# One Trainium2 core, a vision tower kernel: state scan and routed experts as one stage, class key scores in the gate's product

## The reference, cut to what matters

```python
h = h + _L1_attn_ref(_layernorm(h), ...)     # ends in: hs by a scan over the batch axis, y = pad(h) * z; y @ w_out.T
def _L1_ffn_ref(x, W_qkv, b_qkv, W_gate, b_gate, W_experts, b_experts):
    qkv = (x @ W_qkv + b_qkv).reshape(B, S, 3, H, hd)          # 16 heads of 16
    attn = softmax(q k^T / 4) over all 513 tokens of an image
    gate = jax.nn.softmax(x @ W_gate + b_gate, axis=-1)
    top_g, top_i = jax.lax.top_k(gate, TOP_K)                   # 2 of 8
    moe_out = sum over the two of top_g * (x @ W_experts[e] + b_experts[e])
    return attn_out + moe_out
h = h + _L1_ffn_ref(_layernorm(h), ...)
```

## Time and profile before

| | us |
|---|---|
| median of 3 runs (lowest to highest) | 2109.86 (2108.89 to 2119.64) |
| profiled execution: time | 2123.18 |
| profiled execution: span, mean granted clock | 2121.5, 0.941 |
| state scan's result ready | 1310.4 |
| slot table done | 1523.0 |
| first expert product | 1532.9 |
| last bias addition of the expert stage | 1624.8 |

### The profile page before, as it was taken

How to read it: one execution, slowest core, us unless ns; L and a number is a source line. 1 busy time by engine, 2 the same in 40 slices (tenths; PEclk the granted TensorE clock), 3 DMA queues, 4 the chain that set the end, 5 groups by cost and what they waited for, 6 DMA issues and landing times. The chain is left out here.

```text
span 2121.5 us, 37207 instructions
## 1 busy us (share of the span) xinstructions
PE 1915.3 (90%) x10969; PEld 1211.2 (57%) x10969; DVE 1540.5 (73%) x4226; ACT 933.6 (44%) x2148; POOL 991.3 (47%) x1655
## 2 busy tenths in 40 slices
PE   7997997999899998999996994798797899999997
PEld 5886772333788887677774332788674233333332
DVE  3334896776577776899984885787665888898881
ACT  1112564555122222444442442344353277777777
POOL 3553564555333332333332110577444766666662
PEclk9997998999899999999998996899898599999999
DMA  4331667875100001990002001368764134434420
GB/s 132 114 118 39 155 168 182 167 157 109 45 1 1 1 1 71 412 387 1 1 1 61 9 9 30 105 156 232 181 212 140 28 84 97 96 93 93 101 67 27
DMA packets 242423, 216.77 MB, mean 102 GB/s; under 512 B 117762, under 2 KB 216100, under 8 KB 242116
## 3 DMA queue, kind: packets, MB, share of 16 engines
q1 hardware_dynamic: 232596, 188.26, 33.0%
q0 software_dynamic: 9648, 26.36, 3.8%
HBM read 109.35 MB, written 104.82 MB: 101 GB/s over the span
## 5 line engine op out<-in xcount | busy, mean ns | idle before, releaser
L2966 DVE TENSOR_REDUCE attend_mx<-ps 128x1 f32<-128x512 f32 x512 | 320.8, 681 | 38.5 <-PE ps L2620 37.4
L2763 ACT ACTIVATE attend_w<-ps 128x512 f32<-128x512 f32 x512 | 281.8, 596 | 96.9 <-PE ps L2634 94.6
L2620 PE MATMUL ps<-keep_x,keep_o 96*128 96x512 bf16 x512 | 209.3, 414 | 8.2 <-DVE attend_mx L2966 6.4
L2634 PE MATMUL ps<-keep_o,keep_x 99*128 99x512 bf16 x512 | 191.9, 384 | 2.7 <-ACT attend_w L2763 2.7
L2620 PEld LDWEIGHTS ps<-keep_x,keep_o 96*128 96x128 bf16 x512 | 50.2, 98 | 194.5 <-DVE attend_mx L2966 146.2
L981 POOL TENSOR_TENSOR keep_early<-keep_early,first_causal 128x128 f32<-128x128 f32 x256 | 112.9, 456 | 90.8 <-ACT keep_early L949 89.7
L1003 DVE SCALAR_TENSOR_TENSOR keep_early<-ps,first_causal 128x512 f32<-128x512 f32 (+3 forms) x256 | 114.0, 485 | 51.1 <-PE ps L885 46.6
L949 ACT ACTIVATE keep_early<-ps 128x512 f32<-128x512 f32 (+3 forms) x256 | 98.9, 437 | 88.6 <-PE ps L885 88.2
L2652 PE MATMUL ps<-attend_w,keep_early 128*17 128x512 f32 x1024 | 136.3, 601 | 0.0
L1216 PE MATMUL ps<-mlp_zT,keep_early 128*128 128x128 f32 x1056 | 128.0, 280 | 8.0 <-ACT mlp_zT L1258 8.0
L1216 PEld LDWEIGHTS ps<-mlp_zT,keep_early 128*128 128x128 f32 x1056 | 121.8, 194 | 16.0 <-ACT mlp_zT L1258 16.0
(11 more groups left out here) (376 smaller groups left out, 4559.4 us busy)
## 6 DMA issues: line engine op xcount, KB each, us to landing
sorted<-keep_x SPq DMA_DIRECT2D x3, 14720.0 KB, 75.2
tok_xin<-in_xk SPq DMA_DIRECT2D x64, 256.0 KB, 2.6
qk_parts<-qkv_parts SPq DMA_DIRECT2D x33, 384.0 KB, 3.2
qk_parts<-moe_parts SPq DMA_DIRECT2D x33, 384.0 KB, 3.2
keep_o<-qk_parts SPq DMA_DIRECT2D x16, 384.0 KB, 4.5
keep_x<-qk_parts SPq DMA_DIRECT2D x16, 384.0 KB, 5.6
moe_zs<-sorted SPq DMA_DIRECT2D x45, 128.0 KB, 2.4
sorted<-moe_zn POOLq DMA_DIRECT2D x42, 128.0 KB, 2.4
```

The source lines that it names most:

```text
L2620: nc.tensor.matmul(ps[:, MX + i % RING, :], qs[0:R, x.buf(0), h, t * P:(t + 1) * P], ks[0:R, x.buf(0), h, :], start=True, stop=True).then_ ...
L2634: nc.tensor.matmul(ps[:, SC + i % RING, :], ks[:, x.buf(2), HG * g + j, kt * P:(kt + 1) * P], qs[:, x.buf(2), HG * g + j, :], start=True, ...
L2763: nc.scalar.activation(w[:, j, kt % 2, :], ps[:, SC + (HG * k + j) % RING, :], ACT.Exp)\
L2966: nc.vector.tensor_reduce(mx[:, t, k:k + 1], ps[:, MX + (TB * k + t) % RING, :], AX, ALU.max)\
```

## The change

`pass_scan` and `pass_moe` become one pass, `pass_experts`. What it does:

- The scan's buffers are views of `env.o` and `env.x`. The products of a pair of tiles (`carry(p)`) and their addition (`carried(p)`) stand in the turns, one pair every second turn, directly ahead of the pair's statistics. Statistics and deviation work on a pair.
- GpSimd's `deviation` also makes -mean/deviation, and ScalarE normalizes (`normalize`) where VectorE did.
- The class keys times the weights of k and q give 32 columns beside the gate's 8: `class_weights` makes them once (24 instructions on TensorE), and the gate's product of 40 columns gives the class scores too. `class_scores`, `take_class` and `qkf` are gone; `env.cs` holds 40 columns a tile.
- q and k stay in PSUM, in two banks. ScalarE's `first_part` writes the first part from there, VectorE's `remainder` makes the rest from PSUM and that part in four pieces, ScalarE's `second_part` casts, GpSimd's `third` is as before. `v` has four buffers; `rest` and `parts` still two.
- `choose` and `places` read the expert numbers and a zero from PSUM (`IOTA`, `ZERO`), where they read SBUF.
- A projection runs one turn after its gate for i < 8, then two, then three (`projected`), with none in turns 8 and 16; before it was always three.
- The exponents of all tiles are taken at once after the slot table.
- SyncE copies v ahead of the parts. Of the 16 pieces, 8 stay in the turns (tiles 12 to 26, every second one), and 8 stand between the loads of the expert stage.

```diff
+def projected(i):
+    lag = 1 if i < 8 else 2 if i < 16 else 3
+    return None if i in (8, 16) or not 0 <= i - lag < NT else i - lag
 # SyncE
             for s, u, n in tiles():
-                sp.wait_ge(s_p2, s + 1)
-                sp.dma_start(io["qk_parts"]...).then_inc(s_out[u], 16)
                 sp.wait_ge(s_va, s + 1)
...
+                sp.wait_ge(s_p2, s + 1)
+                sp.dma_start(io["qk_parts"]...).then_inc(s_out[u], 16)
+                if s >= 12 and s % 2 == 0 and s < 28:
+                    piece = (s - 12) // 2
+                    env.heads.load_piece(sp, io, 0, piece // 4, piece // 4, piece % 4)
...
                 sp.dma_start(zs[j % NY], io["sorted"][bass.ds(row, P), :]).then_inc(s_zs[j % NY], 16)
+                if j >= 12 and j % 4 == 0 and j < 44:
+                    piece = (j - 12) // 4
+                    env.heads.load_piece(sp, io, 1, piece // 4, 2 + piece // 4, piece % 4)
 # ScalarE
+            def first_part(s):
+                u = s % 2
+                act.wait_ge(s_qk, s + 1)
+                if s == 0:
+                    act.wait_ge(s_kq0, 1)
+                past(act, s_p2, s - 1)
+                past(act, s_out[u], 16 * (s // 2))
+                for n in range(4):
+                    last = nc.scalar.activation(part_at(u, 0, n), ps[:, QK[u], n * P:(n + 1) * P], ACT.Identity, bias=bias_of(n))
+                last.then_inc(s_p0, 1)
+            for i in range(NT + 4):
+                if live(i):
+                    take_zT(i)
+                if i == 2:
+                    take_class_weights()
+                if live(i + 2):
+                    normalize(i + 2)
+                if projected(i - 1) is not None:
+                    second_part(projected(i - 1))
+                if projected(i) is not None:
+                    first_part(projected(i))
 # GpSimd
+            def deviation(p):
+                u, w = (p + 1) % 2, len(members(p))
+                ch = Chain(pool, c_rs, 3 * (p + 1))
+                pool.wait_ge(s_stat, p + 2)
+                past(pool, s_z, 2 * p - 1)
+                ch.link(nc.gpsimd.tensor_tensor(ve[:, u, 0:w], mv[:, u, 0:w, 1], env.eps[:, :].to_broadcast([P, w]), ALU.add))
+                ch.link(nc.gpsimd.tensor_tensor(rs[:, u, 0:w], ve[:, u, 0:w], env.mhalf[:, :].to_broadcast([P, w]), ALU.pow))
+                ch.link(nc.gpsimd.tensor_tensor(nm[:, u, 0:w], mv[:, u, 0:w, 0], rs[:, u, 0:w], ALU.mult))
+                nc.gpsimd.tensor_tensor(nm[:, u, 0:w], no[:, :].to_broadcast([P, w]), nm[:, u, 0:w], ALU.subtract).then_inc(s_rs, 1)
+            for i in range(NT + 4):
+                if i % 2 == 0 and (i + 2) // 2 < NP:
+                    deviation((i + 2) // 2)
+                if live(i - 2):
+                    scatter(i - 2)
+                if projected(i - 1) is not None:
+                    third(projected(i - 1))
 # VectorE
+            def remainder(s):
+                u = s % 2
+                dve.wait_ge(s_p0, s + 1)
+                past(dve, s_p2, s - 1)
+                for n in range(4):
+                    last = nc.vector.scalar_tensor_tensor(rest[:, u, n * P:(n + 1) * P], ps[:, QK[u], n * P:(n + 1) * P], bias_of(n),
+                                                          part_at(u, 0, n), ALU.add, ALU.subtract)
+                last.then_inc(s_rest, 1)
                 if live(i - 1):
                     choose(i - 1)
                 if live(i - 2):
                     places(i - 2)
+                if projected(i - 1) is not None:
+                    remainder(projected(i - 1))
+                if projected(i) is not None:
+                    value(projected(i))
+                if i % 2 == 0 and (i + 2) // 2 < NP:
+                    carried((i + 2) // 2)
+                    stats((i + 2) // 2)
```

More of the change, by code:

```diff
@@ L1830, in _ @@
             convolve(B - 1)
[L1833 to L1915, removed]
-            for u in range(2):
-                batch(u, u)
-            with dve.Fori(1, B // 2) as i:
-                for u in range(2):
-                    batch(2 * i + u, u)
@@ L2000, in pass_moe, with live, members @@
+        s_out, s_vout, s_scat, s_zs, s_yout = (a.sems("out", 2), a.sems("vout", NV), a.sems("scat", NZ), a.sems("zin", NY),
                                                a.sems("yout", NY))
         block = a.block()
-        LATE = 20
-        def each(count):
-            return range(count)
-        def live(t):
-            return 0 <= t < NT
+        U, ABS, EX, LN1, DEL, M, AA, AABS = range(8)
+        BX, HS = U, ABS
+        def live(s):
+            return 0 <= s < NT
+        def members(p):
+            return (0,) if p < 0 else (2 * p + 1, 2 * p + 2)
@@ L2010, in _, with pair_of, part_at, bias_of @@
+        def pair_of(s):
+            return (s - 1) // 2
+        def part_at(u, c, n):
+            return parts[:, u, n % 2, c if n < 2 else SLOTS - 1 - c, :]
+        def bias_of(n):
+            return bias_q[:, n:n + 1] if n < 2 else col(env, "bk1", n - 2)
         @block.sync
         def _(sp):
+            sp.dma_start(x[:, :, :], io["ssm"].rearrange("c r t -> r c t")).then_inc(s_xin, 16)
             sp.dma_start(b_rep[:, :, :].rearrange("p e d -> p (e d)"),
@@ L2047, in _ @@
                 sp.wait_ge(s_out[u], 16 * ((NT + 1 - u) // 2))
[L2048 removed]
+            for w in range(NV):
+                sp.wait_ge(s_vout[w], 16 * ((NT + NV - 1 - w) // NV))
         @block.tensor
@@ L2184, in _, with second_part @@
-            for i in range(NT + 3):
+                if s == 0:
+                    act.wait_ge(s_kq0, 1)
[4 more added lines that the diff above has]
+                last.then_inc(s_p0, 1)
+            def second_part(s):
+                u = s % 2
+                act.wait_ge(s_rest, s + 1)
+                nc.scalar.copy(part_of(parts, u, 1), by_block(rest[:, u, :])).then_inc(s_p1, 1)
@@ L2240, in _ @@
         def _(dve):
+            ch = Chain(dve, c_dve)
+            nc.vector.memset(y0[:, :], 0.0)
             nc.vector.memset(v[:, :, :, :], 1.0)
             nc.vector.memset(one[:, :], 1.0)
-            nc.vector.memset(zero[:, :], 0.0)
+            nc.vector.memset(start[:, 2, :], 0.0)
+            scan.wait(dve)
+            for b in range(B):
+                nc.vector.tensor_scalar(w_b[:, b, :], w_out, group[:, b:b + 1], None, ALU.mult)
             pre.wait(dve)
@@ new lines, in carried, with stats @@
+            def carried(p):
+                dve.wait_ge(s_mm, p + 1)
+                hs = env.h[:, 1 + 2 * p:3 + 2 * p, :]
+                nc.vector.tensor_tensor(hs, ps[:, Y[p % 2], :].rearrange("p (i d) -> p i d", i=2), hs, ALU.add).then_inc(s_h, 1)
+            def stats(p):
+                u = (p + 1) % 2
+                dve.wait_ge(*((s_h, p + 1) if p >= 0 else (s_h0, 1)))
+                past(dve, s_rs, p)
+                for i, s in enumerate(members(p)):
+                    last = nc.vector.bn_stats(st[:, u, i, :], env.h[:, s, :])
+                last.then_inc(c_ln, 1)
+                dve.wait_ge(c_ln, p + 2)
+                nc.vector.memset(env.gap[0:1, :], 0.0)
+                for i, s in enumerate(members(p)):
+                    last = nc.vector.bn_aggr(mv[:, u, i, :], st[:, u, i, :])
+                last.then_inc(s_stat, 1)
```

396 lines of the change are left out of this document (225 added, 171 removed).

## The result

| | before | after |
|---|---|---|
| median, us (lowest to highest, 6 runs each) | 2109.14 (2106.38 to 2119.64) | 2129.48 (2125.69 to 2130.18) |
| ratio, 95% interval | | 1.0081 (1.0065 to 1.0096) |
| profiled execution: span, mean granted clock | 2121.5, 0.941 | 2123.8, 0.938 |

What follows compares the result with a forecast made beforehand. Before, a VectorE-GpSimd loop with a held compare bounds the sort; after, a 12.7 us loop through the parts' landing. Sort +0.2, loads ahead of landings +2, expert stage +11 make +13: 2123 us, range 2090 to 2144.

Steps and rivals of the forecast that it cites:

- The loop: Sort: third part, parts' landing, first part, remainder, value, addition, statistics, deviation form one chain; 12.7 us per two turns, 11 rounds.
- The start: From the scan's result to GpSimd's turn 2: 24.1 us, an estimate good to 3 us.
- The skipped rounds: Sort, turns 8 and 16 without a projection: the loop is broken, and two turns cost about 9 us.
- The end of the sort: From turn 30, no statistics left, through the slot table: 31.0 us, with three rounds of third part to third part.
- loaded landings: Sort: some loads that stay lie ahead of a parts' landing; 2 us added, between 0 and 15.
- Sort in sum: Scan's result to slot table: 212.8 us against 212.6 before, so +0.2, plus 2 us for loads ahead of landings.
- The expert stage: 8 pieces (14 DMAs) added to SyncE's queue, whose issuing is the pace there: +11 us, between 0 and 11.5.
- rival B: Expert stage: the added loads are hidden because SyncE's 1.22 us contains slack; result 2112 us; chance 15%.
- The sum: Whole kernel: +0.2 + 2 + 11 = +13 us, 2123 us on the median.
- What bounded before: Sort before: a 5.50 us turn looped through VectorE and GpSimd, with VectorE's compare held 1.43 us until GpSimd's third part ended.
- Rival A: Sort: GpSimd alone sets the turn, 4.3 us; result 2078 us, or 2100 with half of it; chance 22%.
- Rival C: Sort: TensorE drops to half clock, two turns cost 17 us; +22 if half the rounds suffer, 2145 us; chance 13%.

Runs made afterwards that it cites:

- Experiment 7: The kernel before with the buffer of the bf16 parts three deep and nothing else: 2113.52 us, ratio 1.0005 to the kernel before.
- Experiment 8: The changed kernel with parts three deep, its compare reading the expert numbers from SBUF again: 2081.45 us, ratio 0.9861 to the kernel before.
- experiment 9: The changed kernel with the addition that makes v ahead of the remainder in VectorE's turn: 2124.80 us, ratio 1.0069 to the kernel before.

## Why the prediction was right, point by point

**The loop** was right in mechanism and size. Forecast 12.7 us, measured 12.9. Third part to first part took 3.34 us (forecast 3.28), the landing to deviation 4.4 (forecast 4.4), deviation to third part's end 5.2 (forecast 5.0: the first scatter took 1.03 and not 0.98, the deviation of a pair 1.54 and not 1.38). Three experiments bear on it from different sides: the landing taken out leaves 8.76 (9.17 on the mean), the statistics taken out 9.0 to 11.8, v taken out v's own length. What the sum overlooked is that the rounds that end at turns 8 and 16 have no addition for v, 0.3 us each. The rule of the Trainium skill (DMA: Bandwidth & Descriptors, "Queues, rings and completion order") that the prediction weighed, by which the scatters could have held the landing by about 1.2 us, does not show here: from 1340 to 1425 us the way from third part to first part was 3.32 to 3.35 us where a scatter started 0.16 us behind the third part, and 3.35 to 3.37 where none came for 5.8 us.

**The start**: 23.3, forecast 24.1. **The skipped rounds**: 10.6 and 10.1, forecast 9 each, 2.7 us too low in sum; no run isolates why. **The end of the sort**: 34.8 with everything, forecast 31.0 plus 2 for loaded landings. In it VectorE's operation for the slot table (L2408) took 1.64 us beside GpSimd's third part; in the kernel before it took 0.21.

**Sort in sum**: 220.2, forecast 214.8 with the landings' 2 us. The misses are small: rounds 1.8, skipped rounds 2.7 and the end 1.8 us too low, the start 0.8 too high.

**The expert stage** was right in cause and too high in size. The stretch became 6.8 us longer, the forecast was 11. The term took 1.60 us for a pair of DMAs, from a pair in the sort, and no slack in SyncE. The sign that the prediction named for it, 8 to 12 us longer, did not come; moving the pieces away gave back 6.0. That also takes out rival B (hidden).

**The sum**: +15.0 us in the profiled executions from the scan's result to attention (7.5 + 0.7 + 6.8), forecast +13; by the ratio +17 (14 to 20). The medians 2129.5 and 2109.1 differ by 20; the 2 to 5 us between them and the traces are within what one execution differs from another. Experiment 7, with the same turns as before, had a sort of 210.6 us where the trace of before has 212.6, so some 2 us of them may be the one trace of before; no run assigns the rest. That the sum came so near is in part luck: the sort was forecast 5.4 us too low and the expert stage 4.2 too high, and the two misses nearly cancel.

**What bounded before** was right: the compare held by GpSimd closed the turn. The compare falls from 1.40 (the median up to 1457 us) to 0.16 us when one input comes from PSUM, as the Trainium skill's rule on the shared port (SBUF — State Buffer, "Who interferes with whom") has it. Experiment 8 does not fit it in full: both engines read SBUF in the 11 compares beside the power as well, and none of these was held (0.17 to 0.21 us); there the measurement decides. But what the prediction added, that by this rule 1.43 us a turn return, is far too much: alone it gives 0.35 us a turn in the trace and 0.2% of the time. The rows of before had the limit: GpSimd idles only 0.68 us of a turn, and its own work of 4.8 us is the next bound. **Rival A** (GpSimd alone, 2078 to 2100) was not this kernel, but it was the right picture of what the change can do with a third buffer: 2082.6. **Rival C** did not come: the granted clock was 0.84 to 0.89 in the stretches from 1340 to 1487 us, and the round did not follow it (experiment 9 had 0.83 from 1340 to 1412 us, and shorter rounds).

## What to carry to other kernels

When operations are moved within an engine's turn, ask of each wait what is now queued behind it: here the wait for a buffer's landing cost nothing in the old order (a third buffer there gave 1.0005) and set the whole pace in the new one (a third buffer gave 2.3%). A loop through several engines is found by adding up one round, and tested by taking a single small operation out of it: the round must fall by that operation's own length, and only where the operation stood. And a stall removed alone is worth only the distance to the next bound, 0.35 us a turn of the 1.43 that the row showed. The idle time of the engine that the stall holds up, 0.68 us here, is the most that it can return.
